# Flamingo block with gated cross-attention and experts, 16 batches: batch 0's later key packs split over two queues, batch 1's projections moved, a window table of its own for batch 0, and the last tile of values moved to another step

## What is computed

```python
B, N, D, M, H, Dh = 16, 256, 128, 1601, 16, 8        # batches, tokens, width, context rows, heads
qh = einsum('bnd,hde->bhne', layernorm(x), Wq)
kh = einsum('bmd,hde->bhme', ctx, Wk)
vh = einsum('bmd,hde->bhme', ctx, Wv)
att = softmax(einsum('bhne,bhme->bhnm', qh, kh) * 0.125, axis=-1)
x = x + tanh(g_xattn) * (einsum('bhnm,bhme->bhne', att, vh) joined over heads @ Wo.T)
x = x + tanh(g_ffn) * experts(layernorm(x))          # router softmax, top 2 of 8, gelu
```

## Time and profile before

| what | us |
|---|---|
| median of 3 runs | 1363.93 (1360.14 to 1364.64) |
| profiled execution, its own time | 1353.72 |
| its span | 1351.9 |
| step 0 of batch 0: first score on PE | 47.84 |
| step 8: maxima of group 1 turned | 66.80 |
| step 26: first score of group 2 | 93.30 |
| step 0 of batch 1 | 128.61 |
| length of each later batch up to batch 13 | 70.6 |

### The profile page before, as it was taken

One profiled execution on the slowest core, in us unless ns is written; L12 is line 12 of the kernel. 1 busy time (PEld: TensorE's weight loads), 2 busy tenths in 40 slices (PEclk: granted clock), 3 DMA queues, 4 the chain that ended last, 5 costly groups with the idle time before them and its releaser, 6 DMA issues.

```text
span 1351.9 us, 37790 instructions
## 1 busy us (share of the span) xinstructions
PE 1294.0 (96%) x13888; PEld 626.4 (46%) x13888; DVE 1164.9 (86%) x2268; ACT 1097.9 (81%) x2190; POOL 543.6 (40%) x1208
## 2 busy tenths in 40 slices
PE   5899999999999999999999999999999999999992
PEld 2334444444444444444444444444444444388882
DVE  7788999999999999999999999999999999456444
ACT  2378898988888889898989888898989888965661
POOL 3032526262626253535344444535262603135441
PEclk7699999999999999999999999999999999999997
DMA  3222121212121212122222222121211110187886
GB/s 115 64 84 73 45 69 49 71 48 77 43 82 37 68 50 63 55 63 62 57 66 59 64 60 66 53 67 51 71 47 43 49 48 10 43 260 212 238 242 226
DMA packets 61076, 109.84 MB, mean 81 GB/s; under 512 B 13052, under 2 KB 36476, under 8 KB 60748
## 3 DMA queue, kind: packets, MB, share of 16 engines
q1 hardware_dynamic: 54340, 95.48, 24.3%
q0 software_dynamic: 4320, 8.99, 2.0%
q10 hardware_dynamic: 2232, 2.96, 0.6%
HBM read 49.96 MB, written 13.71 MB: 47 GB/s over the span
## 4 chain that ended last, share of the span: by engine, by line
PE 77%; DVE 17%; issue 3%; DMA 1%; SPq 1%; ACT 1%; POOL 0%; POOLq 0%; DVEq 0%
PE pv L813 28%; PE st L765 14%; DVE mx L1553 14%; PE mxp L787 13%; PE st L1048 5%; PE mxp L1058 4%; PE st L871 4%; PE st L885 3%; PE st L843 1%; PE st L897 1%; PE st L855 1%; PE st L920 1%; PE st L930 1%; DVE x_sb L1748 1%; PE mxp L1023 1%
## 5 line engine op out<-in xcount | busy, mean ns | idle before, releaser
L1553 DVE TENSOR_REDUCE mx<-mxp 128x2 f32<-128x804 f32 x1024 | 985.8, 988 | 70.8 <-PE mxp L787 61.0
L1087 ACT ACTIVATE arena<-st 128x512 f32<-128x512 f32 (+1 forms) x1664 | 891.7, 595 | 85.8 <-PE st L765 79.4
L813 PE MATMUL pv<-arena 128*32 128x256 f32 x6656 | 534.2, 393 | 0.4 <-ACT pv_sb L1094 0.4
L787 PE MATMUL mxp<-kpack,qpack 48*128 48x402 bf16 x2048 | 464.6, 343 | 24.4 <-DVE mx L1553 15.3
L765 PE MATMUL st<-qpack,kpack 51*128 51x256 bf16 (+1 forms) x3328 | 457.9, 273 | 0.2
L765 PEld LDWEIGHTS st<-qpack,kpack 51*128 51x128 bf16 (+1 forms) x3328 | 200.6, 96 | 208.5 <-ACT arena L1087 115.6
L787 PEld LDWEIGHTS mxp<-kpack,qpack 48*128 48x128 bf16 x2048 | 146.0, 93 | 164.1 <-DVE mx L1553 80.8
L813 PEld LDWEIGHTS pv<-arena 128*32 128x32 f32 x6656 | 131.5, 108 | 176.8 <-ACT arena L1087 90.2
L1225 ACT ACTIVATE arena<-st,bias 128x256 f32<-128x256 f32 (+1 forms) x172 | 74.9, 437 | 49.2 <-PE st L1048 46.2
L652 POOL CAST mxs<-nmx 128x8 bf16<-128x8 f32 x64 | 12.2, 191 | 254.5 <-DVE nmx L1561 254.3
L685 POOL DMA_INDIRECT rows<-xrow,pos x64 | 66.0, 1031 | 95.2 <-DVE pos L1410 80.0
(11 more groups left out here) (193 smaller groups left out, 948.7 us busy)
## 6 DMA issues: line engine op xcount, KB each, us to landing
kpack<-ksp SPq DMA_DIRECT2D x762, 50.0 KB
arena<-in_w12T SPq DMA_DIRECT2D x43, 512.0 KB, 4.3
arena<-in_ctxT SPq DMA_DIRECT2D x15, 800.5 KB, 4.4
qpack<-qsp SPq DMA_DIRECT2D x187, 32.0 KB
xblk<-rows SPq DMA_DIRECT2D x28, 132.0 KB, 3.5
rows<-in_pads SPq DMA_DIRECT2D x8, 264.0 KB, 4.4
qpack<-mxT SPq DMA_DIRECT2D x128, 3.0 KB
arena<-results SPq DMA_DIRECT2D x8, 256.0 KB, 7.0
```

The source lines that it names most:

```text
L787: eng.matmul(mxp[pair % MX_BUFS][:, rg, 0:WIN], qpack[rows, b % 2, g * JJ + jj, t * P:(t + 1) * P], kpack[rows, b % 2, g * JJ + jj, WSTART ...
L813: ins = eng.matmul(pv[32 * j:32 * j + 32, 0:N], vaug[0:n, b % 2, kt, at:at + 32], pt[0:n, (2 * u + rg) % PT_BUFS, jj * N:(jj + 1) * N], st ...
L1087: eng.activation(pt[0:n, c % PT_BUFS, :], ring[bank_of["S", u, p]][0:n, :], ACT.Exp, scale=SCALE).then_inc(s_exp, 1)
L1553: eng.tensor_reduce(mx[:, tj, w, :], mxp[windows_done % MX_BUFS][:, :, 0:WIN], AX.X, ALU.max).then_inc(s_red, 1)
```

## The change

It has four parts. Line numbers in this section's rows are those of the file each is from.

1. **Packs of groups 1 to 3 of batch 0.** The twelve DMAs of a group are divided: SP issues the six of `rg` 0, ACT the six of `rg` 1. Group 0's maxima are placed by both, one DMA each. The load of batch 1's context, which stood ahead of group 1's packs on SP, comes behind group 2's; the ones for batch 1 and the load of batch 2's rows move into the steps, to step 9.
2. **Batch 1's preparation.** Its rows and queries are turned ahead of the first window, into PSUM banks that are spare then. Its values leave the start and go to batch 0's steps 25, 26, 27 and 39, where later batches have them too.
3. **A table for batch 0.** `FIRST_WINDOWS_AT` issues one or two windows at the end of each step, none between the scores, from 22 issued at the start; LEAD is 28 where it was 30. Batch 0 then issues 70 windows in its steps where it issued 71. In later batches each step has as many windows as before, but two later in number.
4. **The last tile of values**, for batches 2 and on, is projected at step 39 into the bank that takes the rows (X), where it had a bank of its own at step 28.

The packs of batch 1's keys are divided otherwise too: at step 14 of batch 0 SP packs group 0 and half of group 1 (18 DMAs, before 12), at step 23 the rest of group 1 and group 2 (18, before 24).

```diff
-V_AT = {25: 0, 26: 1, 27: 2, 28: 3}
+V_AT = {25: 0, 26: 1, 27: 2}
-LEAD, SHORT = 30, 7
+FIRST, LEAD = 22, 28
+FIRST_WINDOWS_AT = ("0000000000000000000000000000000000000000000000000000",
+                    "2111211212221111211111211222211111211122111211121112")
@@ issued
-    return LEAD + b * PER_BATCH + ISSUED[2 * r + p] - max(0, SHORT - u // 3)
+    if b == 0:
+        return FIRST + FIRST_ISSUED[2 * r + p]
+    return LEAD + b * PER_BATCH + ISSUED[2 * r + p]
@@ sync
-            eng.dma_start(ctx_sb[:, 1, :], ctxT[1]).then_inc(s_ctx[1], 16)
-            pack_keys(0, 1)
+            def other_keys(g):
+                for part in range(PARTS):
+                    pack_key_rows(eng, 0, g, part, 0)
+            other_keys(1)
             eng.wait_ge(s_kone, 1)
             ones_rows(0)
-            pack_keys(0, 2)
-            place_maxima(0)
-            pack_keys(0, 3)
+            other_keys(2)
+            eng.dma_start(ctx_sb[:, 1, :], ctxT[1]).then_inc(s_ctx[1], 16)
+            other_keys(3)
+            eng.wait_ge(s_mxT, 1)
+            place_half(eng, 0, 0)
             pack_queries(1)
...
-            ones_rows(1)
-            load_rows(2)
...
                     if r == 9:
+                        ones_rows(1)
+                        load_rows(2)
                         load_context(0)
                     elif r == 14:
                         pack_keys(1, 0)
+                        pack_keys(1, 1, range(PARTS // 2))
                     elif r == 23:
-                        pack_keys(1, 1)
+                        pack_keys(1, 1, range(PARTS // 2, PARTS))
                         pack_keys(1, 2)
@@ tensor
+            def last_values(b):
+                i, n = bank_of["X", b + 1], key_rows(KT - 1)
+                eng.matmul(ring[i][0:n, N:N + D], ctx_sb[:, b % 2, M - n:M], wv_sb[:, :], start=True, stop=True
+                           ).then_inc(s_vp, 1)
+                freed[i] = s_v, NV * (b + 1)
...
+            turn_rows("X", 1)
+            queries(1)
             for n in range(issued(0, 0)):
+                if n == 1:
+                    eng.wait_ge(s_xnT, 2)
                 maximum(*divmod(n, NMX))
                 if n == 0:
                     values(0, NV - 1)
-                elif n == X1_AHEAD:
-                    turn_rows("X", 1)
-                elif n == Q1_AHEAD:
-                    queries(1)
-                elif V1_AHEAD <= n < V1_AHEAD + VCH[0][1]:
-                    values(1, 0, [n - V1_AHEAD])
                 elif n == NMX + 1:
                     turn_maxima(0)
-                elif n > NMX + 1 and n - NMX - 1 < NV:
-                    values(1, n - NMX - 1)
@@ scalar
             first_packs(eng, 1)
-            for c in range(NV):
+            copy_rows(1)
+            for c in range(NV - 1):
                 copy_values(0, c)
+            first_queries(1)
+            copy_values(0, NV - 1)
...
-            copy_rows(1)
-            first_queries(1)
-            copy_values(1, 0)
+            for g in range(1, NG):
+                for part in range(PARTS):
+                    pack_key_rows(eng, 0, g, part, 1)
             copy_maxima(0)
-            for c in range(1, NV):
-                copy_values(1, c)
+            eng.wait_ge(s_mxT, 1)
+            place_half(eng, 0, 1)
```

More of the change, by code:

```diff
@@ L107 @@
 ROWS_AT, LAST_ROWS_AT = {1: 40, 2: 42, 3: 44}, {9: 0, 10: 1, 11: 2, 12: 3}
-LEAD, SHORT = 30, 7
+FIRST, LEAD = 22, 28
 WINDOWS_AT = ("1011011110111111111111101001101110011111110111100111",
               "1101111020000000000001101211100011100000011000120000")
+FIRST_WINDOWS_AT = ("0000000000000000000000000000000000000000000000000000",
+                    "2111211212221111211111211222211111211122111211121112")
 PER_BATCH = NG * NMX
-ISSUED = [sum(int(WINDOWS_AT[q][r]) for r in range(UNITS) for q in range(2) if 2 * r + q < c)
-          for c in range(2 * UNITS)]
+ISSUED, FIRST_ISSUED = [[sum(int(at[q][r]) for r in range(UNITS) for q in range(2) if 2 * r + q < c)
+                         for c in range(2 * UNITS)] for at in (WINDOWS_AT, FIRST_WINDOWS_AT)]
 def key_rows(kt):
@@ L145, in prepared @@
         return "K", b + 1, keys_at(b)[r]
-    if 0 < b < B - 1 and r in V_AT:
+    if b + 1 < B and r in V_AT:
         return "V", b + 1, V_AT[r]
@@ L150, in prepared @@
             return kind, b + 2
+    if r == X_AT and b + 1 < B:
+        return "V", b + 1, NV - 1
     return None
@@ L164, in ring_banks @@
         take("V", 0, c)
-    take("X", 1)
-    take("Q", 1)
-    take("V", 1, 0)
     take("M", 0)
-    for c in range(1, NV):
-        take("V", 1, c)
     for u in range(B * UNITS):
@@ L424, in first_packs, with place_half @@
                 pack_query_rows(eng, 0, part, rg)
+        def place_half(eng, G, rg):
+            b, g = divmod(G, NG)
+            r, rows = rg * RSTEP + MAXROW, KINDS * JJ
+            eng.dma_start(qpack[r:r + KINDS, b % 2, g * JJ:(g + 1) * JJ, :],
+                          mxT[rg * rows:(rg + 1) * rows, :]).then_inc(s_mxd[G % 2], 16)
         @block.sync
@@ L451, in place_maxima @@
             def place_maxima(G):
-                b, g = divmod(G, NG)
                 eng.wait_ge(s_mxT, G + 1)
-                rows = KINDS * JJ
                 for rg in range(RG):
-                    r = rg * RSTEP + MAXROW
-                    eng.dma_start(qpack[r:r + KINDS, b % 2, g * JJ:(g + 1) * JJ, :],
-                                  mxT[rg * rows:(rg + 1) * rows, :]).then_inc(s_mxd[G % 2], 16)
+                    place_half(eng, G, rg)
             def load_rows(b):
@@ L803, in weighted @@
                     eng.wait_ge(s_vone, 3)
+                    eng.wait_ge(s_qhi, 2)
                 if r == 0:
@@ L832, in turn_rows @@
             def turn_rows(kind, b):
-                if (kind, b) == ("X", 0):
-                    dst = x0p
+                if kind == "X" and b < 2:
+                    dst = x_first[b]
                 else:
@@ L840, in turn_rows @@
                 eng.wait_ge(s_xn, NT * (norm_no[kind, b] + 1))
+                if kind == "X" and b >= 2:
+                    last_values(b - 1)
                 for t in range(NT):
@@ L846, in queries @@
             def queries(b):
-                if b == 0:
-                    dst = q0p
+                if b < 2:
+                    dst = q_first[b]
                 else:
@@ L872, in keys, with values @@
                            start=True, stop=True).then_inc(s_kp, 1)
-            def values(b, c, some=None):
+            def values(b, c):
                 i = bank_of["V", b, c]
                 t0, tn = VCH[c]
[L878 to L883, removed]
+                eng.wait_ge(*freed[i])
+                for t in range(tn):
                     n = key_rows(t0 + t)
@@ L994, in _ @@
                         keys(b + 1, keys_at(b)[r])
-                    elif b > 0 and r in V_AT:
+                    elif r in V_AT:
                         values(b + 1, V_AT[r])
+                    elif r == X_AT and b + 2 == B:
+                        values(b + 1, NV - 1)
                 if b + 2 < B:
@@ L1096, in copy_rows @@
             def copy_rows(b):
-                src = ring[bank_of["X", b]] if b > 0 else x0p
+                src = ring[bank_of["X", b]] if b > 1 else x_first[b]
                 eng.wait_ge(s_xp, b + 1)
@@ L1103, in first_queries @@
                 if b > 0:
-                    src = ring[bank_of["Q", b]]
+                    src = ring[bank_of["Q", b]] if b > 1 else q_first[b]
                     eng.wait_ge(s_qd[(b - 1) % 2], 16 * PACKS * ((b - 1) // 2 + 1))
@@ L1107, in first_queries @@
                 else:
-                    eng.activation(qsp[:, 0, :], q0p[:, 0:N], ACT.Copy).then_inc(s_qhi, 1)
+                    eng.activation(qsp[:, 0, :], q_first[0][:, 0:N], ACT.Copy).then_inc(s_qhi, 1)
             def first_keys(b, c):
@@ L1121, in first_keys, with copy_last_values @@
                                    ).then_inc(s_khi, 1)
+            def copy_last_values(b):
+                n = key_rows(KT - 1)
+                eng.wait_ge(s_vp, NV * (b + 1))
+                eng.activation(
+                    vaug[0:n, b % 2, KT - 1, 0:VP * H].rearrange("p (h c) -> p h c", c=VP)[:, :, VC:VC + DH],
+                    ring[bank_of["X", b + 1]][0:n, N:N + D].rearrange("p (h e) -> p h e", e=DH), ACT.Copy
+                    ).then_inc(s_v, 1)
             def copy_values(b, c):
@@ L1191, in _ @@
                         first_keys(b + 1, keys_at(b)[r])
-                    elif b > 0 and r in V_AT:
+                    elif r in V_AT:
                         copy_values(b + 1, V_AT[r])
+                    elif r == X_AT and b + 2 == B:
+                        copy_values(b + 1, NV - 1)
                 if b + 2 < B:
@@ L1196, in _ @@
                         copy_rows(b + 2)
+                        copy_last_values(b + 1)
                     elif r == Q_AT:
@@ L1616, in _ @@
```

(2 more changed lines are left out.)

5 lines of the change are left out of this document (2 added, 3 removed).

## The result

The change made the kernel slower: 1379.76 us median of 4 runs (1378.9 to 1380.01) against 1363.34 of 4 runs of the kernel before, measured beside it; ratio 1.013, 95% interval 1.0116 to 1.0144. That is 16.4 us more, where 5.2 less was forecast. The profiled execution took 1379.94, its span 1378.1.

What follows compares the result with a forecast made beforehand. PE was taken to set the pace, DVE close behind, with gains only in the first 129 us. Batch 1 5.6 us earlier, later batches 0, last batch 0.4 later: -5.2, median 1363.9 to 1358.7 us, range 1353.5 to 1362.5.

Steps and rivals of the forecast that it cites:

- Later batches ... I take 0: Batches after batch 1: no change expected, -0.1 to +0.15 us a batch, -1.4 to +2 for 14.
- forecast for the last batch: Last batch: two more windows are left there, 0.4 us later.
- The slower rival: Steady batches lose as PE waits at step 41 for the rows' bank; at 0.7 a batch 1368 us; chance 0.07.
- The moved tile: Steps 28 and 39: the tile takes PE about 0.3 us from one to the other, both PE's, so it cancels.
- the first score: Start of batch 0: first score at 43.6, 4.2 us earlier, with the placement's transfer taken as 1.98.
- the rival of the late ACT queue: Start: packs issued by ACT delay the copy of the maxima; two us lost, 1360.7 us; chance 0.1.
- Here the issue is what SP was late with: Start: SP's issuing of twelve packs for 11.88 us, not transfers, was taken to delay group 0's placement.
- Steps 0 to 8: Batch 0 up to group 1's turn: turn at 57.3, 9.5 us earlier, with PE waiting about 1.8 there.
- Steps 8 to 26: Batch 0 from the turn to group 2's first score: SP's queue decides, 27.7 us against 26.5, step 26 at 85.0.
- Steps 26 on: Rest of batch 0: 38.0 us against 35.3 before, so batch 1 starts 5.6 earlier.
- Sum: Whole kernel: batch 1 starts at 123.0, 5.6 us earlier, plus 0.4 at the end: 5.2 us less.

Runs made afterwards that it cites:

- The first experiment: The kernel before with its windows two later in number (LEAD 28, SHORT 5); 1366.73 against 1352.99 us, ratio 1.0098.
- third: The changed kernel with the last tile of values back at step 28; 1369.4 against 1352.99 us, ratio 1.0115 to the kernel before.
- fourth: The changed kernel with the tile back at step 28 and LEAD 30, two more windows in batch 0's steps; ratio 1.0021 to the kernel before.
- the two last of the changed kernels: The sixth, ratio 1.0005, and the fastest kernel, 1346.84 against 1353.78 us.
- fifth: The fourth with batch 1's packs divided on SP as before the change, 12 at step 14 and 24 at step 23; ratio 0.9974 to the kernel before.
- the second experiment: The kernel before with only the last tile of values moved from step 28 to step 39 (batches 3 on); ratio 1.0028.
- the fastest kernel: The fourth with the edits of the fifth and sixth and group 1's last window issued before the end of step 7; 1346.84 against 1353.78 us, ratio 0.994.
- the sixth: The fourth with group 3's 12 packs all on SP behind the placement of group 0's maxima; ratio 1.0005 to the kernel before.

## Why the prediction was wrong

**First error, the sign: "Later batches ... I take 0".** It asked whether the maxima of a group are ready in time for their turn (they are) and whether the moved tile cancels. It left out that windows with other numbers put the short reductions into other steps. The prediction gave them no cost there; it read only that DVE was busy for 66.31 of 70.66 us, which says nothing of single steps. In steps 2 and 3 DVE had 2.66 of 2.69 us to do, and just ahead of them it had an idle time of 0.64. The step of the prediction that failed is this term: 0 was taken, -1.4 to +2 for all batches given as its bounds, 13 x 1.18 + 0.66 + 1.12 - 0.4 (forecast for the last batch) = 16.7 measured. The first experiment shows it (0.98 of 1.18 from the one number), and the edits of the third and fourth take it back entirely. The slower rival had the right place, the steady batches, and at its 0.7 a batch 1368; it had the wrong cause (the bank held for the rows' turn) and a chance of 0.07. The bank's wait at step 41 does not show: without the moved tile steps 41 and 42 lose as much.

**The moved tile**: "Both steps are PE's, so it should cancel" held for step 39 (+0.33, and -0.11 at the next) and not for step 28: alone, the 0.36 won there is lost by step 34, and in the changed kernel only 0.04 is won. It costs 0.2 a batch, just beyond the upper bound of 0.15.

**Second error, the first score: 43.6 forecast, 47.21 measured.** The issue was at 42.47 for 41.4: ACT's 17 packs took 16.49 us, 0.97 each and not 0.75, so the rival of the late ACT queue happened with 1.1 of its 2 us. The greater part, 2.5 us, is the transfer: I took 1.98 from the earlier trace rows, the last query pack, and behind the key packs of two queues the placements needed 4.65 from issue to landing (47.12, by the trace's semaphore events); the last of group 3's packs had landed at 46.70. With these packs, six of SP's and six of ACT's, taken out of the way it is 2.2, and the first score at 43.46. In two executions of the same start the landing took 4.1 and 5.45. The Trainium skill, page "DMA: Bandwidth & Descriptors", section on issuing engines that are not separate DMA queues, says that DMAs issued by different engines share the same 16 and interleave. The traces agree, 4.65 against 2.2 us; I had cited that rule and then costed the split by its issue time only.

A premise was wrong as well: "Here the issue is what SP was late with". In the kernel before, group 0's maxima had landed at 45.60, and the first score at 47.84 stood in PE's list behind a window that waited for DVE:

```profile
47.66 0.34 PE L787 MATMUL mxp<-kpack,qpack 48*128 48x402 bf16 x2 [0.48 <-DVE mx L1553]
```

So before it was the windows that held the first score, and an earlier placement alone had nothing to win there.

**Steps 0 to 8**: 14.3 from first score to turn, 13.7 forecast; PE waited 1.60 for 1.8 forecast. That window 31 at the end of step 7 is the cause is shown by the two last of the changed kernels: 1.61 with it there, no wait with one window moved from step 7 to step 2.

**Steps 8 to 26**: 27.7 forecast, 29.1 measured, and each part stands in the trace: splits done 12.7 behind the turn (12.4), packs 12.24 (11.8), pads and gap 0.8 (0.7), issue to first score 3.35 (2.8 forecast; again the transfer). The edit with twelve packs confirms that the queue decided. Steps 26 on: 38.4 (38.0).

**Sum**: batch 1 starts at 129.00 for 123.0: 3.6 from the first score, 0.6, 1.4 and 0.4 from the three stretches. Without the steady loss this change would still have been no gain that shows: batch 1 starts at 129.40 by its exponentials, against 129.04 and 127.18 in two executions of the old batch 0. A point that the forecast did not set apart: batch 0 hands over two windows fewer, which makes its end some 1.4 us earlier (third against fourth experiment, from step 26 on), and the later batches pay for it.

**What stays open**: whether the short reductions alone, with every window where it was, would cost the same; why steps 31, 32 and 34 lose together 0.23 to 0.38 in four kernels (28 and 31 ahead, the moved tile, the change) and not in two (29 and 32). DVE's busy share of 8.44 in 8.54 there says that any delay is kept, not where it arises. Open too is the split of step 39's 0.33 between PE and ACT, and whether a position of the moved tile exists that costs nothing; neither was tried.

## What to carry to other kernels

Where two engines both fill a steady loop, an offset is not free because the work per batch is the same: list for each small operation the step into which it falls, and look whether its engine had an idle time behind it there; a busy share over the whole batch can't tell. Ask of a gain at the start whether it was made by leaving work to the loop, and multiply that by the batches. A small DMA on the critical path is costed with what is queued on the DMA engines ahead of it from all queues, and bulk packs that are not yet needed go behind it.

## What the hardware showed unexpectedly

- Packs are slow to issue for a while behind the two DMAs of the ones, whose transfers land from 26.6 to 34.4: two on ACT took 4.31 us, one on SP 3.19, and between 28 and 33 two more on SP 1.66 and 1.13 and one more on ACT 2.28, where an issue of a key pack took 0.60 to 0.79 else. Timeline of the changed kernel:

```profile
26.23 4.31 ACTq L404 DMA_DIRECT2D kpack<-ksp  x2
26.96 3.19 SPq L404 DMA_DIRECT2D kpack<-ksp  x1
```

- The same start differs between executions: the fourth and fifth experiments have one text up to step 14, and their first scores are at 47.61 and 46.38, with the placement issued at 42.07 and 42.18. Two executions with the same batch 0, of the kernel before and of the second experiment, start batch 1 at 129.04 and 127.18. Differences of one microsecond in a first score, and of two in the start of batch 1, say nothing by themselves.
- TensorE's granted clock is 0.50 in the changed kernel up to 53.0, again from 63.3 to 66.7, behind PE's wait of 1.60 at step 8 and the gaps of the first steps, and from 90.6 to 94.0, behind the wait of 3.24 at step 26. In the fastest kernel PE has no wait at these places (0.07 at step 26), and the clock stays at 1.00 from 51.6 to the end of attention. The same wait of 1.60 to 1.61 at step 8 stands in five kernels: in two the clock fell behind it (the changed one and the fourth experiment), in three it did not (the third, the fifth and the sixth). Behind the waits of 3.24 to 4.09 at step 26 it fell in all four that have one.
